# Kernel matrices of the landmarks as row tiles of 32 channels, ahead of the first keys

## What is computed

```python
Q, K, V = project(query)                          # heads: (b, 16, n, 16)
landmarks = K[:, :, landmark_idx, :]
C_Q = _sq_dists(Q, landmarks)                     # max(|x|^2 + |l|^2 - 2 x.l, 0)
C_K = _sq_dists(K, landmarks)
W_sq = C_K[:, :, landmark_idx, :]
Phi_Q, Phi_K = jnp.exp(-C_Q / temperature), jnp.exp(-C_K / temperature)
W_kernel = jnp.exp(-W_sq / temperature) + REG * jnp.eye(NUM_LANDMARKS)
Z = jnp.einsum('bhnk,bhnd->bhkd', Phi_K, V)
Y = jnp.linalg.solve(W_kernel, Z)
out = jnp.einsum('bhnk,bhkd->bhnd', Phi_Q, Y) / norm      # then Wo, layer norm, experts, layer norm
```

## Time and profile before

| | us |
|---|---|
| median of 3 runs | 1769.01 (1767.94 to 1769.63) |
| profiled execution, whole time | 1772.77 |
| profiled execution, span from first to last instruction | 1770.6 |

### The profile page before, as it was taken

The page is one execution under the profiler, slowest core; times in us unless marked ns, Lnnn a source line. Parts: engine busy times, 40 slices in busy tenths (PEclk is TensorE's granted clock), DMA queues, the critical chain, the costliest instruction groups (busy, mean ns, idle before and its releaser), DMA issues.

```text
span 1770.6 us, 47289 instructions
## 1 busy us (share of the span) xinstructions
PE 1372.9 (78%) x17728; PEld 1100.0 (62%) x17728; DVE 1204.2 (68%) x3410; ACT 978.4 (55%) x1699; POOL 833.8 (47%) x929
## 2 busy tenths in 40 slices
PE   3869999998989788898889888887499988882000
PEld 2357787787878556565656666664399888882000
DVE  5768974498843357888887888877666554553766
ACT  2346775676666476676757776764144433331544
POOL 2400000000000027777867787775777777775544
PEclk8689999999999899999989999998699999996555
DMA  3297988776796324544444444433467666675999
GB/s 96 55 195 155 186 188 171 158 171 151 160 191 139 92 87 128 177 138 151 153 158 158 144 144 143 158 123 120 132 211 224 216 213 210 206 226 176 366 338 325
DMA packets 254830, 306.75 MB, mean 173 GB/s; under 512 B 64880, under 2 KB 185968, under 8 KB 254064
## 3 DMA queue, kind: packets, MB, share of 16 engines
q1 hardware_dynamic: 229456, 234.49, 50.4%
q0 software_dynamic: 25152, 69.24, 10.6%
HBM read 150.02 MB, written 96.50 MB: 139 GB/s over the span
## 4 chain that ended last, share of the span: by engine, by line
PE 32%; DVE 24%; POOL 17%; issue 11%; DMA 8%; ACT 5%; SPq 3%; DVEq 0%; POOLq 0%; ACTq 0%
POOL terms_dram L688 7%; PE bank L346 5%; PE bank L347 4%; PE bank L348 4%; POOL rows_dram L678 4%; PE bank L1630 3%; POOL xl L655 2%; DMA out<-phi 2%; DVE phi L1091 2%; PE bank L1646 2%; DVE inversion L1119 2%; PE bank L1631 2%; DVE inversion L1121 1%; DVE phi L1245 1%; POOL rs L646 1%
## 5 line engine op out<-in xcount | busy, mean ns | idle before, releaser
L655 POOL TENSOR_TENSOR xl<-x_raw,xh 128x512 fp32r<-128x512 f32 x60 | 75.9, 1288 | 573.8 <-ACT xh L902 573.4
L678 POOL DMA_INDIRECT rows_dram<-x,place_i x256 | 271.4, 1060 | 104.5 <-issue 69.1
L878 ACT ACTIVATE phi<-bank,nlt,invt 128x512 f32<-128x512 f32 x256 | 185.6, 786 | 60.6 <-PE bank L1743 55.8
L755 ACT ACTIVATE phi<-bank,invt 128x512 f32<-128x512 f32 x256 | 163.1, 685 | 91.9 <-PE bank L1631 91.7
L346 PE MATMUL bank<-weh,kh 128*128 x528 | 162.2, 307 | 26.2 <-DVE kl L1440 25.9
L1440 DVE TENSOR_TENSOR kl<-bank,kh 128x512 fp32r<-128x512 f32 x132 | 91.0, 689 | 117.9 <-ACT kh L951 115.8
L1091 DVE TENSOR_SCALAR phi<-phi,phi_max,phi_min 128x1024 f32<-128x1024 f32 x128 | 103.7, 810 | 97.1 <-ACT phi L755 97.0
L1630 PE MATMUL bank<-l_hh,k_hl 128*128 128x256 f32 x512 | 147.1, 318 | 27.7 <-DMA k_ha<-key_aug 13.9
L348 PE MATMUL bank<-wel,kh 128*128 x528 | 150.3, 285 | 0.0
L347 PE MATMUL bank<-weh,kl 128*128 x528 | 150.1, 284 | 0.0
L1245 DVE TENSOR_SCALAR phi<-phi,phi_max,phi_min 128x1024 f32<-128x1024 f32 x128 | 106.1, 830 | 58.3 <-ACT phi L878 58.1
(11 more groups left out here) (261 smaller groups left out, 4168.6 us busy)
## 6 DMA issues: line engine op xcount, KB each, us to landing
tile_in<-rows_dram SPq DMA_DIRECT2D x264, 130.0 KB
x_raw<-in_xT SPq DMA_DIRECT2D x64, 512.0 KB, 4.7
x_tok<-in_x SPq DMA_DIRECT2D x32, 512.0 KB
attn<-den_dram SPq DMA_DIRECT2D x64, 256.0 KB
phi<-terms_dram SPq DMA_DIRECT2D x22, 512.0 KB, 5.5
out<-phi SPq DMA_DIRECT2D x22, 512.0 KB, 7.5
tile_in<-terms_dram SPq DMA_DIRECT2D x17, 512.0 KB, 7.2
k_hl<-attn_h SPq DMA_DIRECT2D x32, 256.0 KB
```

The lines of the kernel that those rows point to most:

```text
L655: last = nc.gpsimd.tensor_tensor(xl[at][:, k], x_raw[0][:, k], raw(xh[at][:, k]), ALU.subtract)
L678: nc.gpsimd.indirect_dma_start(out=rows_dram, out_offset=bass.IndirectOffsetOnAxis(ap=place_i[:, p % 2, at:at + 1].bitcast(u32), axis=0), ...
L755: nc.scalar.activation(phi[:, n], bank[6 + s][:], ACT.Exp, scale=invt[:]).then_inc(exp_done, 1)
L878: nc.scalar.activation(phi[:, i], bank[4 + i % 4][:], ACT.Exp, bias=nlt[:, c // CPB, i:i + 1], scale=invt[:]).then_inc(qexp_done, 1)
```

## The change

The landmark stage on PE uses tiles of 32 channels (two heads) by 64 landmarks, four at a time, each in a PSUM bank of its own. DVE's `own_blocks` writes, for each batch element, three tiles of 128 x 256: high parts, low parts and squares, each masked to its head within the pair of heads. The norms come from two fp32 products with constants (`minus_pair`, `minus_one`). POOL has no part in the stage, and `bdh`, `bdl` and `augm` are gone; the new tiles lie in `l_hh[1]` and in `phi`. A batch element has four exponentials of 64 x 256 instead of two of 64 x 512, so `W_EXPS` is 4 x `BATCH`. The stage stands ahead of `keys(0)`, `values(0)` and `key_norms(0)` on PE, ACT and DVE. On SP the wait for the end of the landmark distances moves behind `stack_keys(0)`, `stack_norms(0)` and the load of `g3`.

```diff
-                bdh = [sb0(f"bdh{i}", [P, KC, HPS, NL], f32r) for i in range(2)]
-                bdl = [sb0(f"bdl{i}", [P, KC, HPS, NL], f32r) for i in range(2)]
-                augm = [sb0(f"augm{i}", [64, KC, HPS, NL], f32r) for i in range(2)]
+            own_h, own_l = [[l_hh[1][:, 2 * a + i].rearrange("p (s u) k -> p s u k", s=KC) for i in range(2)] for a in range(2)]
+            own_sq = [phi[:, 2, 256 * i:256 * (i + 1)].rearrange("p (s u k) -> p s u k", s=KC, u=2) for i in range(2)]
+            minus_pair, minus_one = phi[:, 3, 0:2 * NL], phi[:, 3, 2 * NL:3 * NL]
...
-        W_EXPS = 2 * BATCH
+        W_EXPS = 4 * BATCH
...
             for i, b in enumerate(W_ORDER):
-                sp.wait_ge(exp_done, 2 * i + 2)
+                sp.wait_ge(exp_done, 4 * i + 4)
...
             load_keys_x(3)
-            sp.wait_ge(dist_done, W_EXPS)
             stack_keys(0)
             stack_norms(0)
             for i in range(2):
                 sp.wait_ge(w_stored[i], 16 * BATCH // 2)
             sp.dma_start(g3, w_dram[:, 0:NH, 0:NH]).then_inc(g_loaded, 16)
+            sp.wait_ge(dist_done, W_EXPS)
             stack_keys(1)
...
             split_hi(1)
+            for i in range(BATCH):
+                if i >= 2:
+                    act.wait_ge(w_stored[i % 2], 16 * (i // 2))
+                for j in range(4):
+                    act.wait_ge(dist_done, 4 * i + j + 1)
+                    nc.scalar.activation(wk_sb[i % 2].rearrange("p s (j u) k -> p j s (u k)", u=2)[:, j],
+                                         bank[4 * (i % 2) + j][0:64, 0:4 * NL].rearrange("p (s n) -> p s n", s=KC),
+                                         ACT.Exp, scale=invt[0:64, :]).then_inc(exp_done, 1)
             keys(0)
...
-            mask = cst[0:32, C_M16:C_M16 + H]
-            for i in range(2):
-                last = V.tensor_copy(augm[i][0:32], rep(mask.rearrange("p (s h) -> p s h", s=KC), 3, NL))
+            V.tensor_scalar(minus_pair.rearrange("p (u k) -> p u k", u=2), rep(cst[:, C_PAIR:C_PAIR + 2], 2, NL), -1.0, None, ALU.mult)
+            V.memset(minus_one, -1.0)
...
+            def own_blocks(b, at):
+
+                pair = rep(rep(cst[:, C_PAIR:C_PAIR + 2], 1, KC), 3, NL)
+                V.tensor_tensor(own_h[at], rep(l2h[:, :, in_batch(b)], 2, 2), pair, ALU.mult)
+                V.tensor_tensor(own_l[at], rep(l2l[:, :, in_batch(b)], 2, 2), pair, ALU.mult)
+                return V.tensor_tensor(own_sq[at], rep(sq[:, :, in_batch(b)], 2, 2), pair, ALU.mult)
...
             for i, b in enumerate(W_ORDER):
                 if i == 1:
                     split_lo(0)
-                if i == 2:
+                if i == 3:
                     split_lo(1)
-                    keys_lo(0)
-                    key_norms(0)
-                if i == 5:
-                    split_lo(2)
                 if i >= 2:
-                    dve.wait_ge(dist_done, 2 * (i - 1))
-                block_hi(b, b % 2).then_inc(bd_ready, 1)
+                    dve.wait_ge(dist_done, 4 * (i - 1))
+                own_blocks(b, i % 2).then_inc(bd_ready, 1)
+            keys_lo(0)
+            key_norms(0)
+            split_lo(2)
             landmark_ones(0)
...
+            def landmark_dists(i, b):
+
+                at, first = i % 2, 4 * (i % 2)
+                wide = lambda a, rows, s: a[rows, s].rearrange("p u k -> p (u k)")
+                for s in range(KC):
+                    cols = slice(2 * NL * s, 2 * NL * (s + 1))
+                    for a, own in ((kh[0], own_h), (kl[0], own_h), (kh[0], own_l)):
+                        for j in range(4):
+                            rows = slice(32 * j, 32 * j + 32)
+                            mm(bank[first + j][0:64, cols], a[rows, s, in_batch(b)], wide(own[at], rows, s),
+                               start=(a is kh[0] and own is own_h), stop=False)
+                    for j in range(4):
+                        rows = slice(32 * j, 32 * j + 32)
+                        mm(bank[first + j][0:64, cols], sq[rows, s, in_batch(b)], minus_pair[rows], start=False, stop=False)
+                    for j in range(4):
+                        rows = slice(32 * j, 32 * j + 32)
+                        last = mm(bank[first + j][0:64, cols], minus_one[rows], wide(own_sq[at], rows, s), start=False, stop=True)
+                        if s == KC - 1:
+                            last.then_inc(dist_done, 1)
...
+            pe.wait_ge(nl_ready, 1)
+            for i, b in enumerate(W_ORDER):
+                pe.wait_ge(bd_ready, i + 1)
+                if i >= 2:
+                    pe.wait_ge(exp_done, 4 * (i - 1))
+                landmark_dists(i, b)
+            pe.wait_ge(exp_done, W_EXPS - 4)
             keys(0, 1)
             for tp in range(2):
                 values(0, tp, 1)
+            pe.wait_ge(exp_done, W_EXPS - 3)
             key_norms(0)
```

More of the change, by code:

```diff
@@ L231, in program @@
         lmT_done, l2_ready, nl_done, nl_ready = sem("lmT_done"), sem("l2_ready"), sem("nl_done"), sem("nl_ready")
-        bd_ready, bdl_ready, w_stored, g_loaded = (
-            sem("bd_ready"), sem("bdl_ready"), [sem(f"w_stored{i}") for i in range(2)], sem("g_loaded"))
+        bd_ready, w_stored, g_loaded = (
+            sem("bd_ready"), [sem(f"w_stored{i}") for i in range(2)], sem("g_loaded"))
         dve_step, pool_step = sem("dve_step"), sem("pool_step")
@@ L625, in _ @@
             last.then_inc(const_set, 1)
[L627 to L640, removed]
             def layernorm_coefs(mv, ve, rs, nt, nm, cols):
@@ L787, in _ @@
             key_norms_hi(0)
[L789 to L797, removed]
+            split_hi(2)
             def save_products(n, dst, scale=1.0):
@@ L1057, in _ @@
             own.then(V.tensor_copy(ln_rows[32:64, BATCH * NL:], raw(augk[0][0:32, 0:NL])))
[L1059 to L1063, removed]
-                    last = V.tensor_tensor(augm[at][32:64, s], rep(ln_rows[32:64, in_batch(b)], 1, HPS),
-                                           rep(cst[32:64, C_M16 + HPS * s:C_M16 + HPS * (s + 1)], 2, NL), ALU.mult)
-                return last
+            def own_blocks(b, at):
[3 more added lines that the diff above has]
+                return V.tensor_tensor(own_sq[at], rep(sq[:, :, in_batch(b)], 2, 2), pair, ALU.mult)
             def landmark_ones(i):
@@ L1576, in _ @@
             pe.wait_ge(setup_done, 1)
-            def key_dists(dst, at, tok, bd, s):
-                wide = lambda a: a.rearrange("p h k -> p (h k)")
-                mm(dst, kh[at][:, s, tok], wide(bdh[bd][:, s]), start=True, stop=False)
-                mm(dst, kl[at][:, s, tok], wide(bdh[bd][:, s]), start=False, stop=False)
-                mm(dst, kh[at][:, s, tok], wide(bdl[bd][:, s]), start=False, stop=False)
-                return mm(dst, augk[at][:, tok], wide(augm[bd][:, s]), start=False, stop=True)
+            def landmark_dists(i, b):
[16 more added lines that the diff above has]
+                            last.then_inc(dist_done, 1)
             def keys(c, at):
@@ L1682, in _ @@
                 values(0, tp, 1)
+            pe.wait_ge(exp_done, W_EXPS - 3)
             key_norms(0)
-            for i, b in enumerate(W_ORDER):
-                pe.wait_ge(bd_ready, i + 1)
-                pe.wait_ge(bdl_ready, i + 1)
-                for s in range(KC):
-                    if i:
-                        pe.wait_ge(exp_done, 2 * i + s - 1)
-                    key_dists(bank[6 + s][0:64, :], 0, slice(b * NL, (b + 1) * NL), b % 2, s).then_inc(dist_done, 1)
-            pe.wait_ge(nl_ready, 1)
             keys(1, 0)
```

7 lines of the change are left out of this document (2 added, 5 removed).

## The result

The changed kernel takes 1746.04 us (median of 8 runs, 1740.42 to 1756.21), the kernel before 1768.47 (median of 8 on the same chip, 1764.87 to 1776.72). The ratio is 0.9874, 95% interval 0.9846 to 0.9901: faster by 1.3%. The forecast was 1745.0. By the medians the gain is 22.4 us, where 24.0 were forecast. The profiled execution took 1744.19, with a span of 1742.1 against 1770.6.

The account below looks back on a forecast made before the run. Everything was taken to wait for the first key distances. Their start moves from 100.8 to 76.8 (62.7 through keys plus 14.1 stack), so 24.0 off the 1769.0 median gives 1745.0 us; range 1739 to 1752, 1736 to 1757 eight times in 10.

Parts of the forecast that it names:

- Start of the stage: PE's first landmark batch, after two DVE copies and three products, was to start at 33.4 us (33.0 to 35.5).
- A batch on PE: One batch element's landmark matmuls on PE: 2.8 us at 1.2 GHz, 1.5 at 2.4 GHz; eight at 2.8 end at 55.8.
- the slow narrow matmuls: Rival: fp32r matmuls of 128 columns in the landmark stage lose their rate; 1759.4 us, or 1752.2 for half; chance 0.13.
- The clock: PE's landmark stage was forecast at the low clock; rival, that it rises there: gain 29.1, time 1739.9 us, chance 0.15.
- The stores: Landmark stage's stores, 3.4 us from issue to landing, allow 2.6 per batch; hidden by 0.2 behind PE's 2.8.
- Keys: Chunk 0's keys on PE right after the landmark stage: 5.5 us, end 61.3; ACT's passes add 1.4, to 62.7.
- The stack: DMA transfers stacking chunk 0's keys before the first distances: 9.8 + 4.3 = 14.1 us (13.0 to 15.7).
- What is late next: DVE's stacked landmarks ready at 73.9, hidden by 2.9 us before the first distances; chunk 0's transfers still end last.
- The loop passes the shift through: After the first distances the order is unchanged and the engines are the limit, so the loop can't absorb the 24.0 us.
- It is the order of the keys that matters: On SP, removing only the stack's wait for landmark distances would gain nothing, since the stack stands behind the stores.
- the gain given back: Rival: the stack is ready earlier but another wait ends last or later clock dips differ; about 1767 us, chance 0.03.
- Serial tiles: Rival: the landmark stage's row tiles run one after another, 11.2 us a batch; about 1812 us, chance 0.06.

Follow-up runs that it names:

- the order alone: Kernel before with only the landmark stage moved ahead of chunk 0's keys, values and norms on PE, ACT and DVE; 1758.10 us, ratio 0.9969.
- the tiles alone: Changed kernel with chunk 0's keys, values and norms put back ahead of the landmark stage; 1749.17 us, ratio 0.9916.
- four buffers: Changed kernel with four buffers of exponentials for the stores instead of two, run twice; 1735.17 and 1863.07 us in different sets, ratios 0.9849 and 0.9832.
- tile by tile: Changed kernel with the same matmuls reordered, all five products of one row tile in a row; 1950.99 us, ratio 1.0304.

## Why the prediction was right

The time was right (1745.0 forecast, 1746.04 measured), and so was the gain at the first distances: 24.0 forecast, 24.0 measured. That the two agree so closely is luck: step by step the forecast is less exact, four errors cancel, and the second execution of the same kernel gained 25.3. The path was right: DMAs into `k_ha` still end last, and what is saved there the loop passes on.

- **Start of the stage**: 33.4 forecast, 33.26 measured. The copies took 0.55 together, the three products 0.34 each instead of 0.42 (DVE starts one before the last has ended); PE starts after the third. That POOL's products lengthen the copies fits the order alone against the tiles alone (above), and the forecast took it from the earlier trace rows.
- **A batch on PE**: 2.8 at the low clock, 1.5 at the high one; measured 3.16 and 1.85, some 0.35 more at either. The fp32 terms were close: a group of four, in 8 records, takes 0.48 to 0.58 (forecast 0.505). The fp32r groups start 0.11 to 0.14 apart, as taken, but from the last of a half's three to the first fp32 one 0.27 pass, so the three take 0.52 instead of 0.39. This term was mis-sized: it was scaled by columns from the earlier trace rows, which has no change of kind in it. No quartet of fp32r came near the 0.43 of the slow narrow matmuls.
- **The clock**: low throughout was forecast, high the rival. It was mixed, and differs between executions of one kernel. The argument from the earlier trace rows, that PE fills 64 columns as before and so stays at 0.50, did not hold: at 37 to 41 the same matmuls ran at 1.00. The Trainium skill (TensorE: Matmul & The Clock Gate, Part 1) says that sustained activity releases the half rate. The second run of four buffers agrees; its first run and tile by tile, busy throughout at 0.50, do not:

```profile
45.00:120.00 75.00, 75.00 (x342) 53.13 (x340) 7.71 (x19) 11.51 (x25) 0.00 (x0) 0.50 0.09 22
```

- **The stores**: forecast to be hidden by 0.2 per batch. This is the step that failed. At the high clock PE needs 1.85 a batch, two batches 3.7, while a buffer's turn takes 1.55 of exponentials, up to 4.5 of landing and the issue, some 5.5 to 6.5 for two. "ACT waiting for a store" was named as a sign of error, and it is in the chain. Against the forecast it cost little, since the faster batches had gained the time that the waits took; against four buffers it costs some 6 us. The keys start at 55.3, forecast 55.8 (-0.5).
- **Keys**: 5.5 forecast at the low clock, 2.9 measured (55.31 to 58.20) at the high one (-2.6). ACT behind them ends 2.35 after PE instead of 1.4, because it was at the last exponentials until 58.26 (+0.9).
- **The stack**: 14.1 forecast, 13.0 to 15.7 as bounds; 16.3 measured (+2.2), the last landing 6.9 instead of 4.3. The load of x was taken as issued 4 us ahead and mostly landed; it was issued at 58.90, 1.7 ahead. The runs above put most of that on the load of x: with it 4.9 ahead the stack took 12.9, with it 2.0 ahead 14.2 to 15.0. The sum of the four is 0.
- **What is late next**: the stacked landmarks' last piece starts at 69.25 and is ready at 70.47, 6.4 us before they are needed (forecast 2.9).

```profile
69.25 1.22 DVE L1059 TENSOR_TENSOR l_lo<-ln_rows,cst 32x1024 fp32r<-32x1024 f32 x1
```

- **The loop passes the shift through**: right (table of chunks). "It is the order of the keys that matters" was half right: the order alone brings 11.6, but the tiles alone 17.2, since the stage, and so the last store, ends earlier whatever the order. Removing SP's wait and nothing else was not tried.
- **The rivals**: the clock did rise, but the stores took the gain; slow narrow matmuls and the gain given back did not come. Serial tiles did not come either, and are one loop order away.

## What to carry to other kernels

When a stage is made much faster, its buffers' turn-round (exponentials, issue, landing) becomes the pace: work it out at the fast clock, not at the slow one, and with landings under the new load. Row tiles paid here only in an order in which neighbours use different rows and banks. And a wait shortened at the first chunk counts only if the second chunk's transfers are earlier too; look at the start of chunk 1 and 4 before believing chunk 0.

## What was not expected of the hardware

- TensorE's clock in one place of one kernel: with PE busy without a pause it stood at 0.50 until about 50 us in one execution and at 1.00 from 37.5 in another. Within the stage it fell only in traces in which PE paused. The loop's dips fall differently as well (mean granted clock 0.96 and 0.92 from 198 to 330), and chunk 16 stands 3.8 us apart in two executions of the same kernel.
- A 64-column copy on DVE took 0.18 alone and 1.02 beside POOL's products, which is more than five times as long.
- The same stack of transfers took 12.5 to 16.3 us (order alone: 13.6, 75.64 to 89.22), mostly depending on how far ahead of it one further load was issued; its last landing 3.2 in the median of the loop and 6.9 here.
- The eight stores landed in 3.4 to 4.5 us when they came 2.9 apart (38.0 to 58.3), and in 3.4 to 3.5 when they came 4.7 apart (50.7 to 83.7, before).
